# Value projections ahead of the value-by-probability products, in the six-layer local-attention stage of a fused decoder kernel

## The reference, cut to what matters

```python
q, k, v = split(shift_tokens(x) @ Wqkv)          # 16 heads of 64
q = rotary(l2norm(q) * qs);  k = rotary_inv(l2norm(k) * ksc)
p = softmax(mask(q @ k.T * 8))                   # windows of 32, with the window before
x = (p @ v) @ Wo + x
xn = layernorm(shift_tokens(x)) * g + b
a, gate = split(xn @ W1 + b1)
x = (a * gelu(gate)) @ W2 + b2 + x
```

## Time and profile before

| what | value |
|---|---|
| median of 3 runs (lowest to highest) | 3261.97 us (3249.2 to 3263.04) |
| the profiled execution: its time, its span | 3251.44 us, 3249.6 us |
| TensorE busy | 3176.8 us, 98% of the span, 51333 matmuls |
| VectorE, ScalarE, GpSimd busy | 2799.0, 2536.8 and 2319.3 us |
| transfers | 310.51 MB, 96 GB/s in the mean |
| mean granted TensorE clock | 0.993 of full |

### The profile page before, as it was taken

The page is one execution under the profiler, slowest core; times in us unless marked ns, Lnnn a source line. Parts: engine busy times, 40 slices in busy tenths (PEclk is TensorE's granted clock), DMA queues, the critical chain, the costliest instruction groups (busy, mean ns, idle before and its releaser), DMA issues.

```text
span 3249.6 us, 125216 instructions
## 1 busy us (share of the span) xinstructions
PE 3176.8 (98%) x51333; PEld 2490.0 (77%) x51333; DVE 2799.0 (86%) x5489; ACT 2536.8 (78%) x5155; POOL 2319.3 (71%) x3895
## 2 busy tenths in 40 slices
PE   8989999899999999999999999999999999999997
PEld 6778787577777777777777777777777777777776
DVE  6844444899999999999999999999999999999996
ACT  5756665588888888888888888888888888888886
POOL 5632222878777777878777777788777877778875
PEclk9999999999999999999999999999999999999998
DMA  4000000655555555556555565555565555555552
GB/s 109 3 7 8 8 8 6 124 117 107 106 107 121 122 107 109 109 115 126 117 107 106 107 124 119 108 109 109 118 129 110 107 106 112 106 114 112 112 114 60
DMA packets 280547, 310.51 MB, mean 96 GB/s; under 512 B 154281, under 2 KB 225582, under 8 KB 279982
## 3 DMA queue, kind: packets, MB, share of 16 engines
q0 software_dynamic: 58368, 201.36, 33.9%
q1 hardware_dynamic: 220892, 100.93, 12.9%
q10 hardware_dynamic: 722, 0.21, 0.0%
HBM read 23.63 MB, written 2.10 MB: 8 GB/s over the span
## 4 chain that ended last, share of the span: by engine, by line
PE 92%; DVE 3%; issue 1%; DMA 1%; POOL 1%; SPq 1%; ACT 1%; DVEq 0%; POOLq 0%; ACTq 0%
PE bank L1182 10%; PE bank L1242 10%; PE bank L1128 10%; PE bank L1160 10%; PE bank L1216 9%; PE bank L1099 7%; PE bank L1231 6%; PE bank L1201 5%; PE bank L1115 5%; PE bank L1139 3%; PE bank L714 2%; PE bank L1196 2%; PE bank L727 2%; PE bank L736 2%; PE bank L791 2%
## 5 line engine op out<-in xcount | busy, mean ns | idle before, releaser
L1420 DVE TENSOR_TENSOR RK<-bank,tables 128x1024 f32<-128x1024 f32 x384 | 467.7, 1220 | 46.5 <-PE bank L1099 46.3
L1406 DVE TENSOR_TENSOR RQ<-bank,q_tables 128x1024 f32<-128x1024 f32 x384 | 451.7, 1218 | 29.2 <-ACT sq L1301 7.4
L1546 POOL DMA_DIRECT2D RK<-RK x192 | 175.9, 916 | 369.4 <-DVE RK L1420 352.2
L1554 POOL TENSOR_TENSOR RK<-RK,rn 128x512 f32<-128x512 f32 x384 | 401.7, 1046 | 36.5 <-DMA RK<-RK 35.5
L1560 POOL TENSOR_TENSOR P<-P,rn 128x512 f32<-128x512 f32 x384 | 403.7, 1051 | 0.0
L1566 POOL TENSOR_TENSOR P<-P,inv_sum 128x512 f32<-128x512 f32 x384 | 394.0, 1047 | 0.0
L1540 POOL DMA_DIRECT2D RQ<-RQ x384 | 387.1, 1310 | 2.3 <-issue 2.3
L1182 PE MATMUL bank<-WV,xcT 128*128 128x512 f32 x768 | 380.5, 618 | 0.0
L1128 PE MATMUL bank<-xcT,WQ 128*128 128x128 f32 x3072 | 374.9, 275 | 3.9 <-ACT xcT L1274 3.9
L1242 PE MATMUL bank<-WO,OT 128*128 128x128 f32 x3072 | 375.4, 275 | 0.0
L1160 PE MATMUL bank<-WA,xcT 128*128 128x512 f32 x768 | 361.6, 593 | 1.8 <-DVE P L1470 1.8
(11 more groups left out here) (167 smaller groups left out, 7449.2 us busy)
## 6 DMA issues: line engine op xcount, KB each, us to landing
RK<-RK POOLq DMA_DIRECT2D x192, 512.0 KB, 5.0
RQ<-RQ POOLq DMA_DIRECT2D x384, 256.0 KB, 6.8
Z<-Z SPq DMA_DIRECT2D x768, 64.0 KB, 4.6
WA<-in_wqkv SPq DMA_DIRECT2D x24, 256.0 KB, 3.0
ystat<-Y SPq DMA_DIRECT2D x192, 32.0 KB
ystat<-Y SPq DMA_DIRECT2D x384, 15.8 KB
ys<-Y SPq DMA_DIRECT2D x192, 32.0 KB
ys<-Y SPq DMA_DIRECT2D x384, 15.8 KB
```

The lines of the kernel that those rows point to most:

```text
L1406: tt(both, src.unsqueeze(1).to_broadcast([128, 2, 8, SEQ]), m.q_tables[:, layer(t), :, :].unsqueeze(2).to_broadcast([128, 2, 8, SEQ]), ALU ...
L1420: tt(both, src.unsqueeze(1).to_broadcast([128, 2, 16, 32]), tab.unsqueeze(2).to_broadcast([128, 2, 16, 32]), ALU.mult).then_inc(s.rotated. ...
L1554: tt(part, part, wide(m.rn[:, t % 4, 16 + 8 * j:24 + 8 * j]), ALU.mult).then_inc(s.k_scaled.sem, 1)
```

## The change

The two value projections move ahead of the products, with the turning of the query lengths between them, so that the products stand right before the scores. The orders of the other engines change with it, and the semaphores follow these orders. On SP the move into `ys` goes from the head of the turn to behind the next turn's start: `ff_input(i - 6)`, `probs_moved(i - 4)`, `layer_input(i + 1)`, where it was `ff_input(i - 5)`, `layer_input(i + 1)`, with `probs_moved(i - 3)` last. Nothing that is computed changes. The diff, cut (the counted orders follow the new sequences: `squared` and `rotated` become Q0 Q1 K0 K1, `v` and `v_copied` 0 1, `less` 1 0, and each wait names the part that is now last):

```diff
 # SP: weights(i)
                 if 2 <= n < 6:
-                    at_least(sp, s.v.sem, s.v.upto(0, first))
+                    at_least(sp, s.v.sem, s.v.upto(1, first))
...
                 if n == TILES - 1:
-                    sp.wait_ge(s.v.sem, s.v.upto(0, first + TILES))
+                    sp.wait_ge(s.v.sem, s.v.upto(1, first + TILES))
 # SP: the loop
-        for i in range(N + LAST + 1):
-            ff_input(i - 5)
+        for i in range(N + LAST + 2):
+            ff_input(i - 6)
+            probs_moved(i - 4)
             layer_input(i + 1)
-            store(i - LAST - (N - TILES))
+            store(i - LAST - 1 - (N - TILES))
             if i < N:
                 weights(i)
-            probs_moved(i - 3)
 # PE: values(t, j)
-                if j == 1:
+                if j == 0:
                     pe.wait_ge(m.w_v, 16 * layer(t) + 16)
+                    at_least(pe, s.k_copied.sem, s.k_copied.upto(0, t))
+                else:
                     at_least(pe, s.xn_copied, t - 5)
...
-                else:
-                    at_least(pe, s.k_copied.sem, s.k_copied.upto(0, t))
 # PE: the loop
             keys(i, 0)
+            keys_turned(i - 1, 1)
+            ff_out(i - 8)
+            query_lengths(i)
+            keys_turned(i - 1, 0)
             keys(i, 1)
-            keys_turned(i - 1, 1)
-            query_lengths(i)
-            ff_out(i - 8)
-            keys_turned(i - 1, 0)
+            normal_turned(i - 6)
+            values(i, 0)
             query_lengths_turned(i)
-            normal_turned(i - 6)
+            values(i, 1)
             head_outputs(i - 4)
-            values(i, 1)
-            values(i, 0)
             scores(i - 1)
 # ACT: values_out(t, bb)
+                if bb == 0:
+                    at_least(act, s.o, 2 * (t - 3))
 # ACT: the loop
             squares(i, QUERIES, 1)
+            squares(i, KEYS, 0)
             normalised(i - 6)
             keys_out(i - 1, 1)
+            keys_out(i - 1, 0)
+            query_lengths_out(i)
+            normal_out(i - 6)
             squares(i, KEYS, 1)
-            query_lengths_out(i)
-            squares(i, KEYS, 0)
-            normal_out(i - 6)
-            keys_out(i - 1, 0)
             exponents(i - 2, 1)
-            values_out(i, 1)
+            exponents(i - 2, 0)
+            values_out(i, 0)
             outputs_out(i - 4, 1)
-            values_out(i, 0)
             outputs_out(i - 4, 0)
             seeded(i)
-            exponents(i - 2, 0)
+            values_out(i, 1)
 # DVE: the loop
             ff_added(i - 8)
+            key_rotary(i, 0)
             key_rotary(i, 1)
             query_floor(i)
-            key_rotary(i, 0)
             squares_summed(i)
+            key_floor(i)
             statistics(i - 5)
-            key_floor(i)
             probs_turned(i - 3, 1)
             probs_turned(i - 3, 0)
+            row_sums(i - 2, 1)
             maximum(i - 1, 1)
             maximum(i - 1, 0)
-            less_maximum(i - 1, 0)
-            row_sums(i - 2, 1)
+            row_sums(i - 2, 0)
+            attention_added(i - 4)
             less_maximum(i - 1, 1)
             inverse_sums(i - 2, 1)
-            attention_added(i - 4)
             gated(i - 7)
-            row_sums(i - 2, 0)
+            less_maximum(i - 1, 0)
             inverse_sums(i - 2, 0)
 # GpSimd: the loop
             inverse_lengths(i)
+            keys_scaled(i, 1)
             mean_shift(i - 5)
-            keys_scaled(i, 1)
+            keys_scaled(i, 0)
             scores_scaled(i - 1, 0)
-            keys_scaled(i, 0)
             scores_scaled(i - 1, 1)
```

More of the change, by code:

```diff
@@ L994, in local @@
     s.x_turned, s.x_copied = sem("local_x_turned"), sem("local_x_copied")
-    s.qk, s.squared, s.rotated = counted("qk", *four), counted("squared", (QUERIES, 0), (QUERIES, 1), (KEYS, 1), (KEYS, 0)), counted("rotated", (QUERIES, 0), (QUERIES, 1), (KEYS, 1), (KEYS, 0))
+    s.qk, s.squared, s.rotated = counted("qk", *four), counted("squared", *four), counted("rotated", *four)
     s.summed, s.k_floor = sem("local_summed"), sem("local_k_floor")
@@ L1002, in local @@
     s.k_turned, s.k_copied = counted("k_turned", 1, 0), counted("k_copied", 1, 0)
-    s.v, s.v_copied = counted("v", 1, 0), counted("v_copied", 1, 0)
-    s.scores, s.mx, s.less = sem("local_scores"), counted("mx", 1, 0), counted("less", 0, 1)
+    s.v, s.v_copied = counted("v", 0, 1), counted("v_copied", 0, 1)
+    s.scores, s.mx, s.less = sem("local_scores"), counted("mx", 1, 0), counted("less", 1, 0)
     s.scaled, s.probs, s.row_sum = counted("scaled", 0, 1), counted("probs", 1, 0), counted("row_sum", 1, 0)
@@ L1191, in scores @@
                 if t == N - 1:
-                    pe.wait_ge(s.less.sem, s.less.upto(1, t))
+                    pe.wait_ge(s.less.sem, s.less.upto(0, t))
                 crossed = ((0, 0), (1, 1), (0, 1), (1, 0))
@@ L1222, in head_outputs @@
                 pe.wait_ge(s.p_moved[t % 2], 64 * (t // 2) + 64)
-                pe.wait_ge(s.v_copied.sem, s.v_copied.upto(0, t + 1))
+                pe.wait_ge(s.v_copied.sem, s.v_copied.upto(1, t + 1))
                 pe.wait_ge(s.k_copied.sem, s.k_copied.upto(1, min(t + 4, N)))
@@ L1303, in squares @@
                 else:
-                    if half == 1:
+                    if half == 0:
                         at_least(act, s.summed, t)
@@ L1359, in _ @@
             squares(i, QUERIES, 1)
+            squares(i, KEYS, 0)
+            if i == 0:
+                m.cross_tail()
             normalised(i - 6)
             keys_out(i - 1, 1)
+            keys_out(i - 1, 0)
+            query_lengths_out(i)
+            normal_out(i - 6)
             squares(i, KEYS, 1)
-            if i == 0:
-                m.cross_tail()
-            query_lengths_out(i)
-            squares(i, KEYS, 0)
-            normal_out(i - 6)
-            keys_out(i - 1, 0)
             exponents(i - 2, 1)
-            values_out(i, 1)
+            exponents(i - 2, 0)
+            values_out(i, 0)
             outputs_out(i - 4, 1)
-            values_out(i, 0)
             outputs_out(i - 4, 0)
             seeded(i)
-            exponents(i - 2, 0)
+            values_out(i, 1)
             if i % TILES == 20 and i + TILES < N:
@@ L1446, in squares_summed @@
             if exists(t):
-                dve.wait_ge(s.squared.sem, s.squared.upto((KEYS, 0), t + 1))
+                dve.wait_ge(s.squared.sem, s.squared.upto((KEYS, 1), t + 1))
                 nc.vector.tensor_reduce(m.ss[:, t % 2, :], m.sq[:, KEYS, :].rearrange("p (h d) -> p h d", d=HD), AX.X,
@@ L1544, in keys_added @@
             if exists(t):
-                pool.wait_ge(s.rotated.sem, s.rotated.upto((KEYS, 0), t + 1))
+                pool.wait_ge(s.rotated.sem, s.rotated.upto((KEYS, 1), t + 1))
                 pool.dma_start(m.RK[:, 0, :], m.RK[:, 1, :], accum_op=ALU.add).then_inc(s.k_added, 16)
```

## The result

| | before | after |
|---|---|---|
| median (lowest to highest), 4 runs | 3261.14 us (3249.2 to 3263.04) | 3296.84 us (3288.32 to 3300.5) |
| ratio to before, 95% interval | | 1.0115 (1.0099 to 1.0132) |
| span of the profiled execution | 3249.6 us | 3293.3 us |
| mean granted TensorE clock | 0.993 | 0.983 |

What follows compares the result with a forecast made beforehand. TensorE was taken as the bound, busy 499.7 of 500 us. Terms -59 + 2 + 2 + 40 + 21 + 3 + 15 = +24 us gave 3275 or, on the median, 3286; 3280 was taken, range 3225 to 3315.

Steps and rivals of the forecast that it cites:

- ten stalls behind two waiting loads: Layer boundaries, sync queue: ys stands behind waiting W1 and WV loads, five stalls each, 40 and 21 us; chance 0.50.
- WV: Turn 31, layers 0 to 4: ys behind WV's load lands at 16.3 us, loss 4.2 us, five times 21.
- the clock: At ten boundary stalls TensorE's clock falls to its lower level: 1.5 us each, 15 us (0 to 34).
- The joints: TensorE, 188 turns: one leaving and one entering of 64x64 work gone, 0.30 us a turn, 56 us.
- The doubt whether products and mask join at no cost: Joint of products and scores on TensorE: if it costs an entry again, 0.09 us, the gain is 39 us.
- The other engines keep up: Plain turn of 13.43 us: VectorE holds, with 0.6 us idle ahead of the second key half; cost 0.
- W1: Turn 6, layers 1 to 5: ys behind W1's load lands at 20.0 us, loss 7.9 us, five times 40.
- Z's 4.6: Time from issue to landing taken for ys from Z on the same queue: 4.6 us in the middle, 2.3 to 7.0.
- T - 12.1: PE's loss in us behind WV's load, T being when ys lands in the turn; 4.2 us for 16.3.
- The rest: Small costs on PE: key copy 2 us, GpSimd's uneven landings 2, loads of turns 2 to 5, 8 and 9, 3.
- The last layer: Last layer: VectorE's extra addition hides its wait for the second key half's squares, another 3 us gained.

Runs made afterwards that it cites:

- fifth experiment: The change with ys ahead of the weights, and PE's second value run put back between products and scores: 3248.5 us, ratio 0.9969 to the kernel before.
- first two experiments: The changed kernel with ys ahead of weights(i) in every turn: 3209.37 us, 0.9859; with that only in turn 6 of each layer: 3252.33 us, 0.9991.
- seventh experiment: The changed kernel, ys ahead of weights only in each layer's turn 6, WV's load for layers 1 to 5 cut to 16 KB: 3239.3 us, 0.9951.

## Why the prediction was right, point by point

The forecast of 3280 us and of a slower kernel holds; 3296.84 lies in the range. The mechanism was right: ten stalls behind two waiting loads, at the turns named. The number owes something to luck. The sum was +24 us on the profiled execution, measured are +43.7, and errors of both signs lie between: WV cost 12 us more than forecast and the unevenness 13 more, the clock 6 less. By its steps:

1. **The joints.** Forecast: a turn of 13.43 us, 188 x 0.30 = 56 us. Measured: 13.42 and 0.32, 60 us. The doubt whether products and mask join at no cost is settled: they do. The fifth experiment shows that the step is this and nothing else.
2. **The other engines keep up.** Right: no engine gives TensorE a regular wait in the plain turn. VectorE's idle time before the second key half is 0.47 us in turn 38; forecast was 0.6.
3. **W1.** Forecast: issue 13.6 into the turn, ys at 14.0, 14.6 and 15.4, statistics at 20.0, 7.9 us each, 40 in sum. Measured: 13.6; 14.1, 15.2 and 16.8; 20.1 to 20.3; 44.2 in sum with the clock's part. That 20.0 was met is partly luck: the last issue came 1.4 us later than forecast, and the flight behind it was 3.1 to 3.5 us where Z's 4.6 was taken. The first two experiments show the cause and its size.
4. **WV.** The place and the load's time (9.8 forecast, 9.85 measured) were right, the size was not. Forecast was a landing at 16.3 and 21 us in sum; measured are 17.9 to 19.4 and 38.4. The failing term is ys's flight, for which I took Z's middle value, 4.6 us; from the last issue to the statistics it took 6.1 to 7.2 here, over Z's longest, 7.0, in three of the five turns. The seventh experiment sets the load's own bytes at 1 us of it. With the measured landings my own formula T - 12.1 gives 6.6 us on average, 33 in sum; the other 5 us fit the clock.
5. **The clock.** It fell as forecast, in all ten places, but cost less than the 15 us taken. In turn 39 the queries take 3.57 us (1096.93 - 1093.36) instead of 1.79, yet the key projection behind them had to wait for VectorE until 1096.6 anyway: 0.3 us. Behind WV in turn 32 two key matmuls still run slowly (993.09 to 994.71 is 1.62 us for what takes 0.86). What is left of each long turn after T - 12.1 is 0.4 to 1.7 us, 9 us in all (82.5 less 40 and 33). That all of it is the clock isn't shown, so 9 us is the most it can be. Windows of the kernel after (the last column but two is the granted clock):

```profile
1087.00:1093.20 6.20, 0.00 (x0) 0.00 (x0) 1.62 (x5) 0.87 (x3) 0.38 (x2) 0.76 0.54 115
1093.20:1097.00 3.80, 3.65 (x17) 3.65 (x18) 3.80 (x10) 3.74 (x8) 3.15 (x10) 0.50 0.29 66
1097.00:1101.00 4.00, 4.00 (x36) 2.59 (x35) 4.00 (x8) 3.15 (x8) 3.59 (x4) 1.00 0.16 35
```

6. **The rest.** Forecast: 7 us for key copy, GpSimd's landings and the other loads. Measured: 25 us of unevenness, 2.5 before. This step missed a mechanism, the gaps in the scores: 20 of them with 8.8 us of idle time in the view of waits. The 21 turns that have one are 16.3 us over the commonest.
7. **The last layer.** The 3 us there were misread. Of the 3.2 us of idle time in the earlier trace rows, 2.6 lie behind 3176, the last input turning. TensorE's waits for VectorE in turns 168 to 191 (2857 to 3176) were 1.4 us (in total, times, longest):

```profile
PE bank L1196 <- DVE RK L1420: 1.4, 5, 0.4
```

   They did go, down to 0.2 us after and to none in the fifth experiment. But two gaps in the scores came instead, so these turns have 3.9 us over the commonest after, 2.5 before.

The two stages before the third, which the change doesn't touch, took 4.3 us more in the profiled execution of after (the first input turning stands at 564.6 and 560.3); 3.5 and 1.5 us are won in the first eight turns and behind the last. From the table: -58 for 183 shorter turns, 82.5 for the ten, 25 - 5 for the others over before's, which with these three gives 44.

The Trainium skill (TensorEngine Tiling (Array Packing), Key Properties) says that a change of the tiling mode drains the array. The turns of before, after and the fifth experiment agree in that a change costs time, and put a number to it: one change into and one out of 64x64 tiles together cost 0.32 us.

The version that beats both kernels is the first experiment's: the change with ys ahead of the weights, 3209.37 us, 1.4% under before.

## What to carry to other kernels

A steady turn can gain, and the kernel lose, at the few turns that aren't plain. In a queue where moves and weight loads stand in one order, look for each load that waits, and ask what is behind it and who needs that in the same turn: here one line's place was worth 2.6%. And where an order is shortened by joining dense stretches, price the gain by the joints alone, then measure the joint by itself.

## What the runs showed of the hardware

- TensorE can run out of instructions in a dense stretch. With products and scores adjoining (264 instructions in 2.2 us), gaps appear at a fixed place of the instruction stream: after the 183rd matmul of a turn (0.4 to 1.0 us from start to start); with 24 more instructions ahead of the loop after the 203rd (0.4 to 1.1); with 16 more after the 206th (0.3 to 0.7); and none when 0.95 us of value matmuls stand between the two. A 16 KB packet of instructions ended 1.25 to 1.52 us before the matmul behind each of the 21 gaps of the kernel after. They were 21 in that kernel and 5 in the first experiment's, with the same PE program, by whether that packet started later than 9.4 us into the turn.
- A short transfer (64 KB in three pieces) that was issued as GpSimd's accumulating transfers began was followed by the statistics that wait for it 6.1 to 7.2 us after its last issue (5.1 to 6.3 with no large load ahead of it). Issued 4 to 5 us later, behind W1, it took 3.1 to 3.5.
- A stall of TensorE of 4.3 to 6.6 us brought its granted clock to 0.50 in all ten places. It fell in the stall, in one place 0.2 us after it, and stayed there until 3.4 to 6.2 us after the stall. What that costs depends on who waits next: 0.3 us in turn 39, at most 1.7 us in any of the ten.
